# AFM tower on one core: the first tile's store, and the second tile's gathers, held until two steps have been multiplied

## The chip, the cores and the metric

The kernel runs on one core of one Trainium2 chip. The metric is the device time of one execution in microseconds (us); lower is better. The profile is of one execution of its own, so each reading of a trace is set against the time of that execution.

## What is computed

There are 1024 samples with 33 fields. Each field's id picks a row of 128 numbers from the field's own table. All 528 pairs of fields are multiplied elementwise, projected by a 128 x 128 matrix, put through a relu and reduced to one score a pair; a softmax over the pairs weighs the pair products, and a small MLP with three matrices follows. Cut to what matters:

```python
e = jnp.stack([tbl_0[ids[:, 0]], ..., tbl_32[ids[:, 32]]], axis=1)     # 1024 x 33 x 128, float32
row, col = np.triu_indices(33, k=1)
inner = e[:, row] * e[:, col]                                          # 1024 x 528 x 128
fm = relu(einsum('bpd,ad->bpa', inner, attn_W) + attn_b)
attn = softmax(einsum('ba,bpa->bp', gnn_feature, fm), axis=1)
pooled = einsum('bp,bpd->bd', attn, inner) * 100.0
h = concatenate([gnn_feature, pooled, gnn_feature], axis=1)
h = relu(h @ W_top1 + b_top1)
h = relu(h @ W_top2 + b_top2)
y = h @ W_top3
```

## The kernel before, in words

The 1024 samples are cut into eight tiles of 128 samples, and a tile into 32 steps of 4 samples: 256 steps in all. Steps are what the engines are busy with from about a twentieth of the time on.

**Rows of a tile.** GpSimd issues 33 indirect DMAs a tile (`gather(t)`, L280), one a field, each of which puts 128 rows of 512 bytes into `x_rows`. They are in five chunks c of 8, 8, 8, 8 and 1 fields, each with its own semaphore. Before a chunk of tile t > 0 is gathered, GpSimd waits until the tile before has been transposed out of that part of `x_rows` (`s_xt_done`) and until the rows of the tile before have been stored (`s_store`, 16 a store). SyncE stores all of `x_rows`, 2112 KB, to `x_dram` in device memory once all five chunks have landed (`store_rows(t)`, L230). TensorE turns a chunk over, field by field (`transpose_x(t, c)`, L620), ScalarE copies the result into `xt` (L347), and for the first two chunks copies it once more within `xt` (L337). There is one `x_rows`, and two halves of `xt`, used by turns.

**A step S.** VectorE writes 2112 columns of pair products (`product(S)`, L418). ScalarE rounds most of them to a short form (`round_inner`, L316), VectorE subtracts it to get the rest (`rest_of_inner`, L423). TensorE multiplies the 2112 columns in five chunks (`hidden(S)`), one or two of them in full precision (L580) and the others in three passes of parts (L587, L588, L589); steps 0 and 1 have four and three chunks in full precision. Each finished chunk adds 1 to `s_hidden`, so a step adds `CHUNKS`, which is 5. ScalarE applies the relu, two chunks at a time (L308). Every second step TensorE reduces two steps of `fm` to scores (L610, 32 matmuls). Products have four buffers: `product(S)` waits for `hidden(S - 4)`.

**Other work** of a tile is spread over the steps of the next by fixed lists: at steps 7, 10, 13 and 16 the weighted sums of the tile before (`fields`, L634, which read `x_fields`, loaded by SyncE from `x_dram`, and `attn_t`, spread by SyncE), at steps 18, 20, 22, 24 and 26 the transposes of the tile after (L620), at 19, 21 and 23 the MLP.

**The start.** Tile 0 has nothing before it: its five chunks are gathered, transposed and copied, and `product(0)` on VectorE waits for the last copy (`s_xt_out`). Then the steps begin.

**SyncE's queue**, in order: loads of ids, weights and biases; `store_rows(0)`; `store_rows(1)`; a wait for the first store and eight loads of `x_fields` (L219) for tile 0; then for each tile, as its attention gets ready, eight spreads of `attn_t` (L224), loads and spreads of the other two quarters, `store_rows(t + 2)`, and the loads for tile t + 1.

Of the kernel before, what the change touches and what calls it, by code (L numbers as in the profile page):

```python
# [12 lines left out]
def afm_tower(nc, gnn, ids, tables, w1, b1, w2, b2, w3, attn_w, attn_b, out):  # L13
# [12 lines left out]
    CHUNKS = 5  # L26
# [24 lines left out]
    FIELDS_AT = (7, 10, 13, 16)  # L51
    XT_AT = (18, 20, 22, 24, 26)
    MLP_AT = (19, 21, 23)
    MAX_AT, EXP_AT, INV_AT, SCALE_AT, TURN_AT = 1, 2, 2, 3, 4


# [8 lines left out]
    def jobs_of(S):  # L65
# [4 lines left out]
        if s in XT_AT and t + 1 < T:  # L70
            jobs.append(("x_t", t + 1, XT_AT.index(s)))
        if s in MLP_AT and t > 0:
            jobs.append(("mlp", t - 1, MLP_AT.index(s)))
        if S in LAST_FIELDS_AT:
# [12 lines left out]
    with ctx:  # L87
# [6 lines left out]
        def sem(name):  # L94
            return ctx.enter_context(nc.semaphore(name))
# [61 lines left out]
        s_hidden = sem("hidden_ready")  # L157
# [37 lines left out]
        def fields_in(c):  # L195
            return min(FU, F - FU * c)
# [16 lines left out]
        @block.sync  # L213
        def _(sp):
            def load_fields(t, c, dst, signal):
                for q in range(QS):
                    first = t * P + QS * FN * c + q
                    rows = x_dram[first:first + QS * (FN - 1) + 1:QS, 1:F, :]
                    sp.dma_start(dst[q * I:(q + 1) * I], rows.rearrange("n f d -> f n d")).then_inc(signal, 16)  # L219

            def spread_attn(c):
                for q in range(QS):
                    own = slice(q * I, (q + 1) * I)
                    sp.dma_start(attn_t[own, c % 2, q], attn_turned[own, c * FN:(c + 1) * FN, :])\  # L224
                        .then_inc(s_spread[c % 2], 16)

            def store_rows(t):
                for c in range(XJ):
                    sp.wait_ge(s_gather[c], 16 * fields_in(c) * (t + 1))
                sp.dma_start(x_dram[t * P:(t + 1) * P, :, :], x_rows[:]).then_inc(s_store, 16)  # L230

            sp.dma_start(ids_all[:], ids.rearrange("(t p) f -> p t f", p=P)).then_inc(s_ids, 16)
            sp.dma_start(attn_w_rows, attn_w).then_inc(s_small, 16)
            sp.dma_start(gnn_rows, gnn.rearrange("(t p) a -> p t a", p=P)).then_inc(s_small, 16)
            sp.dma_start(attn_b_sb[:], attn_b.rearrange("(a n) -> a n", n=1), allow_slow_non_contiguous=True).then_inc(s_small, 16)
            sp.dma_start(w1_sb[:], w1[0:2 * P, :].rearrange("(k p) n -> p k n", p=P)).then_inc(s_weights, 16)
            sp.dma_start(h1[:].rearrange("p m b -> p (m b)"), w1[2 * P:3 * P, :]).then_inc(s_weights, 16)
            sp.dma_start(w2_sb[:], w2.rearrange("(k p) n -> p k n", p=P)).then_inc(s_weights, 16)
            sp.dma_start(w3_sb[:], w3.rearrange("(k p) n -> p (k n)", p=P), allow_slow_non_contiguous=True).then_inc(s_weights, 16)
            sp.dma_start(b1_sb[:], b1.rearrange("(m p) -> p m", p=P), allow_slow_non_contiguous=True).then_inc(s_weights, 16)  # L240
            sp.dma_start(b2_sb[:], b2.rearrange("(m p) -> p m", p=P), allow_slow_non_contiguous=True).then_inc(s_weights, 16)
            store_rows(0)
            store_rows(1)
            sp.wait_ge(s_setup_t, 2)
            sp.wait_ge(s_store, 16)
            load_fields(0, 0, x_fields[:, 0], s_fields[0])
            load_fields(0, 1, x_fields[:, 1], s_fields[1])
            for t in range(T - 1):
                sp.wait_ge(s_inv, 3 * (t + 1))
                spread_attn(0)  # L250
                spread_attn(1)
                for c in (2, 3):
                    sp.wait_ge(s_fields_done, FJ * t + c - 1)
                    load_fields(t, c, x_fields[:, c % 2], s_fields[c % 2])
                    spread_attn(c)
                if t + 2 < T:
                    store_rows(t + 2)
                sp.wait_ge(s_store, 16 * (t + 2))
                for c in (0, 1):
                    sp.wait_ge(s_fields_done, FJ * t + c + 3)  # L260
                    load_fields(t + 1, c, x_fields[:, c], s_fields[c])
            sp.wait_ge(s_inv, 3 * T)
            spread_attn(0)
            spread_attn(1)
            sp.wait_ge(s_fields_done, FJ * (T - 1) + 1)
            load_fields(T - 1, 2, x_fields[:, 0], s_fields[0])
            spread_attn(2)
            sp.wait_ge(s_fields_done, FJ * (T - 1) + 2)
            load_fields(T - 1, 3, x_fields[:, 1], s_fields[1])
            sp.wait_ge(s_out, 16 * T)  # L270
# [135 lines left out]
        def _(dve):  # L406
# [123 lines left out]
            for S in range(ALL):  # L530
                t, s = divmod(S, STEPS)
                if S + 1 < ALL:
                    rest_of_inner(S + 1)
                weighs = [job for job in (jobs_of(S - 1) if S > 0 else []) if job[0] == "fields"]
                for _, of, c in weighs:
                    weigh(of, c)
                if part_at(S, TURN_AT) is not None:
                    turn_attn(part_at(S, TURN_AT))
                if S + 3 < ALL:
                    if (S + 3) % STEPS == 0:  # L540
                        dve.wait_ge(s_xt_out, XJ * (t + 2))
                        dve.wait_ge(s_repeat, K // FU * (t + 2))
                    product(S + 3)
                for _, of, c in weighs:
                    sum_weighted(of, c)
                if part_at(S, MAX_AT) is not None:
                    row_max(part_at(S, MAX_AT))
                if s == MAX_AT and t > 0:
                    gnn_block(t)
                if part_at(S, INV_AT) is not None:  # L550
                    invert_sum(part_at(S, INV_AT))
# [170 lines left out]
```

## Time and profile before

| | us |
|---|---|
| median of 3 runs | 1270.39 |
| lowest and highest | 1270.38, 1270.89 |
| the profiled execution | 1270.63 |
| its span, first to last instruction | 1268.2 |
| TensorE busy | 1201.0 (95%) |
| VectorE busy | 1147.9 (91%) |
| ScalarE busy | 1018.7 (80%) |
| GpSimd busy | 451.8 (36%) |

Times in the rows are microseconds from the span's start. A row of the order of time gives start, duration, engine, line, operation, output and inputs, shapes and a count (merged instructions); in brackets it gives how long the engine had been idle before, and what released it. SPq is SyncE issuing a DMA, PE is TensorE, PEld its weight loads, DVE VectorE, ACT ScalarE, POOL GpSimd. The ends of matmuls are modelled by the profiler, not observed. "remote" is the page's name for a releaser that it could match to no instruction.

### The profile page before, as it was taken

The numbers are of one execution on the slowest core, as the hardware profiler recorded it, in microseconds if no ns is written. First come the engines' busy times: TensorE is split into PE (matmuls) and PEld (weight loads), VectorE is DVE, ScalarE is ACT, GpSimd is POOL, SyncE is SP. The second block draws the span as 40 slices with busy tenths as digits, with TensorE's granted clock in tenths as the row PEclk, the third lists the DMA queues.
The fourth block names the chain that finished last, engine by engine and source line by source line (L and its number), as shares of the span: only waits on it lengthen the run. The fifth ranks groups of instructions, "written<-read, shape, count | busy, mean of one in ns | idle before, by whom it ended". The sixth has DMA issues, their size and how long they took to land.

```text
span 1268.2 us, 20736 instructions
## 1 busy us (share of the span) xinstructions
PE 1201.0 (95%) x8732; PEld 898.7 (71%) x8732; DVE 1147.9 (91%) x649; ACT 1018.7 (80%) x1039; POOL 451.8 (36%) x270
## 2 busy tenths in 40 slices
PE   1499999999999999999999999999999999999998
PEld 1267676777777777777777777677777777777766
DVE  2399899998999989999899989999799998999994
ACT  1288898778987889878897798978888788887883
POOL 6587684018800386005840088201880000000000
PEclk9999999999999999999999999999999999999999
DMA  4211410311103111131101311031110300011001
GB/s 108 97 34 50 105 32 26 102 45 30 34 13 125 31 32 28 30 106 37 32 20 47 106 27 32 20 111 39 30 34 21 117 18 1 1 29 39 17 9 38
DMA packets 54859, 58.83 MB, mean 46 GB/s; under 512 B 10728, under 2 KB 49136, under 8 KB 53744
## 3 DMA queue, kind: packets, MB, share of 16 engines
q1 hardware_dynamic: 46304, 40.20, 10.4%
q0 software_dynamic: 8448, 17.32, 5.2%
q8 instruction: 69, 1.13, 0.4%
q14 instruction: 22, 0.18, 0.0%
q10 hardware_dynamic: 16, 0.00, 0.0%
HBM read 36.12 MB, written 17.31 MB: 42 GB/s over the span
## 4 chain that ended last, share of the span: by engine, by line
PE 83%; ACT 8%; issue 4%; DVE 2%; POOL 2%; another core or an unknown queue 1%; DMA 1%; SPq 0%; ACTq 0%; DVEq 0%; POOLq 0%
PE scores L610 19%; PE ring L580 17%; PE ring L587 13%; PE ring L589 12%; PE ring L588 12%; PE ring L634 4%; ACT fm L308 3%; ACT inner_hi L316 3%; PE ring L620 2%; POOL x_rows L280 2%; PE ring L654 1%; DVE products L418 1%; ACT exp_pairs L323 1%; PE ring L648 1%
## 5 line engine op out<-in xcount | busy, mean ns | idle before, releaser
L308 ACT ACTIVATE fm<-ring,attn_b_sb 128x848 f32<-128x848 f32 (+1 forms) x640 | 597.2, 971 | 183.1 <-PE ring L580 174.3
L418 DVE TENSOR_TENSOR products<-xt 128x2112 f32<-128x2112 f32 x256 | 601.9, 2351 | 37.1 <-ACT xt L347 37.1
L280 POOL DMA_INDIRECT x_rows<-in_tbl,ids_all x264 | 451.1, 1709 | 498.2 <-PE ring L620 408.3
L423 DVE TENSOR_TENSOR low_parts<-products,inner_hi 128x1688 fp32r<-128x1688 f32 (+4 forms) x256 | 467.1, 1825 | 57.1 <-ACT inner_hi L316 56.0
L587 PE MATMUL ring<-inner_hi,attn_wt_lo 128*128 128x424 f32 (+1 forms) x971 | 433.1, 446 | 5.1 <-ACT fm L308 5.1
L316 ACT CAST inner_hi<-products 128x1688 fp32r<-128x1688 f32 (+4 forms) x256 | 392.3, 1532 | 5.2 <-DVE products L418 5.2
L589 PE MATMUL ring<-inner_hi,attn_wt_hi 128*128 128x424 f32 (+1 forms) x971 | 344.1, 354 | 0.0
L588 PE MATMUL ring<-low_parts,attn_wt_hi 128*128 128x424 f32 (+1 forms) x971 | 343.7, 354 | 0.0
L580 PE MATMUL ring<-products,attn_wt 128*128 128x424 f32 (+1 forms) x618 | 275.8, 542 | 10.0 <-issue 6.4
L610 PE MATMUL scores<-fm,gnn_blocks 128*32 128x264 f32 x4096 | 254.6, 389 | 6.5 <-ACT exp_pairs L323 6.4
L587 PEld LDWEIGHTS ring<-inner_hi,attn_wt_lo 128*128 128x128 f32 x971 | 182.6, 188 | 70.8 <-issue 37.6
L588 PEld LDWEIGHTS ring<-low_parts,attn_wt_hi 128*128 128x128 f32 x971 | 183.0, 188 | 43.5 <-issue 40.1
L610 PEld LDWEIGHTS scores<-fm,gnn_blocks 128*32 128x32 f32 x4096 | 120.0, 109 | 107.7 <-issue 13.8
L589 PEld LDWEIGHTS ring<-inner_hi,attn_wt_hi 128*128 128x128 f32 x971 | 182.4, 188 | 5.2
L580 PEld LDWEIGHTS ring<-products,attn_wt 128*128 128x128 f32 x618 | 104.6, 190 | 85.4 <-issue 78.2
L620 PE MATMUL ring<-ident,x_rows 128*128 128x128 f32 x264 | 39.2, 292 | 34.0 <-DMA x_rows<-in_tbl,ids_all 31.1
L634 PE MATMUL ring<-attn_t,x_fields 128*128 128x128 f32 x512 | 62.5, 275 | 2.0 <-ACT attn_t L401 1.4
L634 PEld LDWEIGHTS ring<-attn_t,x_fields 128*128 128x128 f32 x512 | 61.8, 191 | 3.2 <-issue 3.1
L347 ACT COPY xt<-ring 128x1024 f32<-128x1024 f32 (+1 forms) x40 | 38.5, 964 | 31.3 <-PE ring L620 15.7
L620 PEld LDWEIGHTS ring<-ident,x_rows 128*128 128x128 f32 x264 | 33.0, 151 | 39.4 <-DMA x_rows<-in_tbl,ids_all 25.7
L473 DVE TENSOR_TENSOR attn<-ring,xt 128x1024 f32<-128x1024 f32 x30 | 36.6, 1220 | 2.8 <-PE ring L634 2.8
L481 DVE TENSOR_REDUCE pooled<-attn 128x32 f32<-128x1024 f32 x30 | 36.5, 1216 | 0.1
(53 smaller groups left out, 203.9 us busy)
## 6 DMA issues: line engine op xcount, KB each, us to landing
x_dram<-x_rows SPq DMA_DIRECT2D x8, 2112.0 KB, 6.6
x_fields<-x_dram SPq DMA_DIRECT2D x128, 128.0 KB
x_rows<-in_tbl,ids_all POOLq DMA_INDIRECT x264
attn_t<-attn_turned SPq DMA_DIRECT2D x124, 32.0 KB, 1.9
w_sb<-in_W_top SPq DMA_DIRECT2D x2, 512.0 KB
x_fields<-in_r_gnn_feature SPq DMA_DIRECT2D x1, 512.0 KB
h<-in_W_top SPq DMA_DIRECT2D x1, 256.0 KB
ids_all<-in_ids SPq DMA_DIRECT2D x1, 132.0 KB, 2.7
```

Of the source, the lines that this page charges most:

```text
L280: nc.gpsimd.indirect_dma_start(out=x_rows[:, f, :], out_offset=None, in_=tables[f], in_offset=bass.IndirectOffsetOnAxis(ap=ids_all[:, t, f ...
L308: nc.scalar.activation(dst, slot(("hidden", pair, j))[:, :, 0:n], ACT.Relu, bias=attn_b_sb[:, 0:1]).then_inc(s_fm, 1)
L316: nc.scalar.copy(inner_hi[:, S % HI_BUFS, 0:COLS - at], plain[:, S % INNER_BUFS, at:]).then_inc(s_hi, 1)
L418: nc.vector.tensor_tensor(dst, a, b, ALU.mult).then_inc(s_inner, 1)
L423: nc.vector.tensor_tensor(inner[:, S % INNER_BUFS, at:end], plain[:, S % INNER_BUFS, at:end], inner_hi[:, S % HI_BUFS, 0:end - at].bitcast ...
L580: nc.tensor.matmul(dst, attn_wt[:], plain[:, S % INNER_BUFS, begin:end], start=True, stop=True)\
L587: nc.tensor.matmul(dst, attn_wt_lo[:], hi, start=True, stop=False)
L588: nc.tensor.matmul(dst, attn_wt_hi[:], lo, start=False, stop=False)
L589: nc.tensor.matmul(dst, attn_wt_hi[:], hi, start=False, stop=True).then_inc(s_hidden, 1)
L610: last = nc.tensor.matmul(scores[I * j:I * j + I, h, 0:HALF], block_of(s, j), fm[:, S % FM_BUFS, at:at + HALF], start=s == 0, stop=s == ST ...
L620: last = nc.tensor.transpose(to[:, n // 4, n % 4 * P:(n % 4 + 1) * P], x_rows[:, FU * c + n, :], ident[:])
L634: last = nc.tensor.matmul(bank[:, h, to:to + QS * I], x[:, n, :], own[:, :, n, :], start=True, stop=True)
```

## The change

One constant and one wait. SyncE, before it looks at the gathers of tile 0, waits until `s_hidden` has reached 10, that is, until all ten chunks of steps 0 and 1 have been multiplied. Everything behind that wait in SyncE's queue is behind it too: the first two stores and the loads of `x_fields` for tile 0. The gathers of tile 1 wait for the first store in GpSimd's queue and move with it. Nothing is added to any other engine, and no instruction is removed.

```diff
@@ -51,6 +51,7 @@
     FIELDS_AT = (7, 10, 13, 16)
     XT_AT = (18, 20, 22, 24, 26)
     MLP_AT = (19, 21, 23)
+    QUIET = 2
     MAX_AT, EXP_AT, INV_AT, SCALE_AT, TURN_AT = 1, 2, 2, 3, 4
 
 
@@ -239,6 +240,7 @@
             sp.dma_start(b2_sb[:], b2.rearrange("(m p) -> p m", p=P), allow_slow_non_contiguous=True).then_inc(s_weights, 16)
+            sp.wait_ge(s_hidden, CHUNKS * QUIET)
             store_rows(0)
             store_rows(1)
             sp.wait_ge(s_setup_t, 2)
```

## Rows read from the trace of the kernel before

**Rows 1.** The page's chain that ended last, and its tenths of busy time.

```profile
PE   1499999999999999999999999999999999999998
DVE  2399899998999989999899989999799998999994
...
PE 83%; ACT 8%; issue 4%; DVE 2%; POOL 2%; another core or an unknown queue 1%; DMA 1%; SPq 0%; ACTq 0%; DVEq 0%; POOLq 0%
```

**Rows 2.** The chain of waits in order of time, 39 to 76 us: start, us, what.

```profile
39.08 11.84 another core or an unknown queue
50.92 1.35 ACT xt L347 x2
52.29 4.63 DVE products L418 x2
...
60.64 2.28 DVE products L418
62.95 1.61 ACT inner_hi L316
64.56 0.87 ACT fm L308
67.46 1.92 PE scores L610 x32
...
75.61 1.92 PE scores L610 x32
```

**Rows 3.** TensorE in order of time: bursts of transposes, first steps.

```profile
15.86 1.94 PE L620 MATMUL ring<-ident,x_rows 128*128 128x128 f32 x8 [6.65 <-DMA x_rows<-in_tbl,ids_all]
26.07 1.97 PE L620 MATMUL ring<-ident,x_rows 128*128 128x128 f32 x8 [8.28 <-DMA x_rows<-in_tbl,ids_all]
35.99 1.97 PE L620 MATMUL ring<-ident,x_rows 128*128 128x128 f32 x8 [7.95 <-DMA x_rows<-in_tbl,ids_all]
46.19 2.18 PE L620 MATMUL ring<-ident,x_rows 128*128 128x128 f32 x9 [8.22 <-DMA x_rows<-in_tbl,ids_all]
...
54.75 5.12 PE L580 MATMUL ring<-products,attn_wt 128*128 128x424 f32 x8 [6.38 <-issue]
...
60.28 2.28 PE L580 MATMUL ring<-products,attn_wt 128*128 128x416 f32 x6
...
63.36 0.35 PE L589 MATMUL ring<-inner_hi,attn_wt_hi 128*128 128x424 f32 x1
...
65.47 0.46 PE L587 MATMUL ring<-inner_hi,attn_wt_lo 128*128 128x424 f32 x1 [0.34 <-ACT fm L308]
```

**Rows 4.** ScalarE in order of time: the copies into `xt`.

```profile
17.84 1.08 ACT L347 COPY xt<-ring 128x1024 f32<-128x1024 f32 x1 [3.80 <-issue]
...
28.08 1.08 ACT L347 COPY xt<-ring 128x1024 f32<-128x1024 f32 x1 [8.01 <-PE ring L620]
...
38.00 1.08 ACT L347 COPY xt<-ring 128x1024 f32<-128x1024 f32 x1 [7.68 <-PE ring L620]
50.91 1.35 ACT L347 COPY xt<-ring 128x1024 f32<-128x1024 f32 x2 [11.83 <-remote]
```

**Rows 5.** SyncE and GpSimd in order of time: stores, loads, first and last gathers of tiles 1, 2.

```profile
47.43 0.34 SPq L230 DMA_DIRECT2D x_dram<-x_rows  x1
...
54.63 3.11 POOL L280 DMA_INDIRECT x_rows<-in_tbl,ids_all  x1 [8.88 <-DMA x_dram<-x_rows]
58.04 2.46 POOL L280 DMA_INDIRECT x_rows<-in_tbl,ids_all  x1 [0.30 <-issue]
60.81 2.91 POOL L280 DMA_INDIRECT x_rows<-in_tbl,ids_all  x1 [0.30 <-issue]
...
71.80 1.52 POOL L280 DMA_INDIRECT x_rows<-in_tbl,ids_all  x1 [0.30 <-issue]
...
121.12 1.96 POOL L280 DMA_INDIRECT x_rows<-in_tbl,ids_all  x1 [0.30 <-issue]
...
124.70 0.33 SPq L230 DMA_DIRECT2D x_dram<-x_rows  x1
125.14 6.88 SPq L219 DMA_DIRECT2D x_fields<-x_dram  x8
...
134.50 0.94 POOL L280 DMA_INDIRECT x_rows<-in_tbl,ids_all  x1 [11.42 <-PE ring L620]
...
203.31 4.67 POOL L280 DMA_INDIRECT x_rows<-in_tbl,ids_all  x1 [0.30 <-issue]
...
281.54 2.37 POOL L280 DMA_INDIRECT x_rows<-in_tbl,ids_all  x1 [73.56 <-PE ring L620]
```

**Rows 6.** Stretches of the first store: engines, clock, DMA share, GB/s.

```profile
core 0: us, PE busy (x) PEld busy (x) DVE busy (x) ACT busy (x) POOL busy (x), PEclk, DMA share, GB/s
48.20:50.90 2.70, 0.17 (x1) 0.00 (x0) 0.00 (x0) 0.00 (x0) 0.00 (x0) 1.00 1.11 469
```

**Rows 7.** The same view for two later stores, in full stride.

```profile
248.50:255.10 6.60, 6.60 (x54) 4.62 (x53) 6.60 (x5) 5.33 (x7) 0.00 (x0) 1.00 0.80 333
398.60:405.20 6.60, 6.60 (x54) 4.62 (x53) 6.60 (x5) 5.33 (x7) 0.00 (x0) 1.00 0.81 333
```

**Rows 8.** VectorE in order of time: the same product of tiles 1, 2 and 7.

```profile
199.84 2.35 DVE L418 TENSOR_TENSOR products<-xt 128x2112 f32<-128x2112 f32 x1
...
349.81 2.35 DVE L418 TENSOR_TENSOR products<-xt 128x2112 f32<-128x2112 f32 x1
...
1099.82 2.35 DVE L418 TENSOR_TENSOR products<-xt 128x2112 f32<-128x2112 f32 x1
```

**Rows 9.** TensorE in order of time: transposes for tile 1.

```profile
133.20 1.03 PE L620 MATMUL ring<-ident,x_rows 128*128 128x128 f32 x8
...
143.67 1.06 PE L620 MATMUL ring<-ident,x_rows 128*128 128x128 f32 x8 [0.76 <-ACT fm L308]
```

**Rows 10.** `x_rows` and `x_dram`: transposes' range of starts, issue to landing up to 140 us.

```profile
L620 PE MATMUL ring<-ident,x_rows x66: 270/361/475, 15.9 to 172.2; 128*128 128x128 f32 x66
...
DMA to landing us min/median/max: 6.4/7.2/8.0
```

**Rows 11.** Weighted sums for tile 0: TensorE's matmuls and the spreads, range of starts.

```profile
L634 PE MATMUL ring<-attn_t,x_fields x48: 270/275/275, 228.5 to 258.8; 128*128 128x128 f32 x48
L224 SPq DMA_DIRECT2D attn_t<-attn_turned x16: 512/590/603, 216.0 to 247.7; - x16
```

## The prediction

> **What bounds the kernel now.** I read the page's chain that ended last first [rows 1]: 83% of it is TensorE, and the tenths show both TensorE and VectorE at 9 in nearly every slice after the second. A change to one store and to gathers can only matter if it moves the moment at which this dense part begins, or disturbs it. So I went on to the chain in order of time [rows 2]. Up to 39 us it is gathers and the transposes behind them; then come 11.84 us put down to "another core or an unknown queue", then ScalarE's last two copies into `xt`, then VectorE's first products. The reader is to see the odd entry: there is no other core, and the copies should be waiting for the transposes.
>
> TensorE and ScalarE in order of time show what is hidden in it. In the first three bursts of eight transposes ScalarE starts 0.04 us after the modelled end: 15.86 + 1.94 = 17.80 and 17.84, 26.07 + 1.97 = 28.04 and 28.08, 35.99 + 1.97 = 37.96 and 38.00 [rows 3, 4]. The fourth burst has nine, the eighth of which should end at 46.19 + 1.97 = 48.16, so the copy is due at 48.20. It starts at 50.91, released by "remote" [rows 4]. **2.71 us are lost** there, and only there. In those 2.7 us every engine is idle but the DMA engines, which run at 469 GB/s: this is the first store, issued at 47.43 [rows 5, 6]. 47.43 is the only store that meets the end of a burst of transposes.
>
> From `product(0)` at 52.29 VectorE does not wait again in the opening, and through product 3, the rounding and a relu it leads to TensorE's restart at 65.47, after which TensorE is dense: reductions at 67.46 and 75.61 [rows 2, 3]. So a shift of 52.29 is a shift of everything.
>
> **Does such a shift survive to the end?** The same product of tiles 1, 2 and 7 starts at 199.84, 349.81 and 1099.82 [rows 8]: 149.97 us for one tile and 750.01 / 5 = 150.00 for each of the next five, although tiles 1 to 6 have gathers in them and the last one has no more to fetch. No step in the dense part waits for a fixed moment; what is won at 52.29 is won at the end. By the same rows gathers and stores in full stride cost nothing measurable.
>
> **The change, part by part.**
>
> The added wait itself: one instruction on SyncE, which has been waiting anyway; nothing runs on it but issues. Zero, hidden behind the loads of the start, and the issue of a store is no busy time of another engine.
>
> The store of tile 0 leaves 47.43. If it is what held the transposes' result back, the copy starts at 48.20, `product(0)` at 52.29 - 2.71 = 49.58, TensorE at 54.75 - 2.71 = 52.04. The gain is 2.71 us. Below, it is bounded by nothing (0, the stall is not the store's); above, by what an earlier start of TensorE could bring besides. TensorE's first eight full-precision matmuls take 5.12 us, 0.64 each, and the next six 2.28 us, 0.38 each [rows 3]: it is at 1.2 GHz first and at 2.4 GHz from about 59 us on. Shifted by 2.71 us it may rise sooner or later against the work. That moves TensorE by about 1 us either way (three or four matmuls at 0.64 in place of 0.38), but what it restarts on at 65.47 is ScalarE's relu, fed by VectorE [rows 2, 3], with 0.34 us to spare. So I allow 0.7 us of further gain and 0.7 us of loss, and take 0 as the likeliest.
>
> The store now starts when step 1 is multiplied. The last matmul of step 1 ends at 63.36 + 0.35 = 63.71 now [rows 3], at 61.0 after the shift. It lands 6.4 to 8.0 us later [rows 10], under steps 2 and 3. What does it cost there? Two later stores in full stride have TensorE and VectorE busy 6.60 of 6.60 us [rows 7]: zero. I take this, the nearest row, with one doubt, priced below.
>
> The gathers of tile 1 begin 54.63 - 47.43 = 7.20 us after the store's issue now [rows 5], so at 68.2, up to 69.8 for a slow landing: 14 to 15 us later. Eight of them end at 71.80 + 1.52 = 73.3 now, 88 at the latest; the first transposes of tile 1 want them at 133.20 - 2.7 = 130.5 [rows 5, 9]. All 33 end at 121.12 + 1.96 = 123.1 now, at 134 to 138 then (the first three take 3.11, 2.46 and 2.91 beside 1.5 to 2 of the later ones, so some of the delay is made good); the fifth chunk is wanted at 172.2 - 2.7 = 169.5 [rows 5, 10]. Spare time over 30 us: zero.
>
> Behind it in SyncE's queue: `store_rows(1)` goes from 124.70 to about 136 to 140, and the eight loads of `x_fields` with it, from 125.14 [rows 5]. They are wanted at 228.5 [rows 11]. Zero. The spreads that are queued behind start at 216.0 [rows 11], far later. In GpSimd's queue the gathers of tile 2 now wait for `store_rows(1)` to land, at 143 to 148 instead of 134.50; their last, 203.31, goes to 212 to 220 [rows 5], and they are wanted by transposes that end at 281.5 [rows 5]. Zero. `store_rows(2)` is held by SyncE's own order, and its window at 248.5 is far behind the gathers. From tile 2 on the schedule is the old one, 2.71 us earlier.
>
> **The sum**, against the profiled execution: 1270.63 - 2.71 = 1267.92. That execution is 0.24 above the median of the runs shown, so in medians 1270.39 - 2.71 = 1267.7. A measurement of this kernel can tell about 0.2% from no change, 2.54 us; the forecast gain is just above that.
>
> The Trainium skill speaks against the cause that I assume: its page "SBUF — State Buffer", in "SBUF: two separate sides", says that engine ports and DMA ports are disjoint, so that a DMA can't be slowed by a compute operation nor the other way round, and that TensorE and ScalarE never wait on anyone. Rows 7 agree with it, rows 6 look as if they did not. By that rule the sum would be 1270.4, no change. Its page "Perfetto Trace Analysis", in "Tensor Engine Instruction (MATMUL, LD_WEIGHTS)", adds that a matmul's end is estimated and that the semaphore goes out only when the write has been acknowledged; so the 48.16 above is a model, and 50.91 the first real sign of the end.
>
> **The rivals.**
>
> *The stall is not the store's and stays.* For it: two stores in full stride disturb nothing [rows 7], and the onset is one coincidence. Against it: three bursts without a store have 0.04 us, the one with a store 2.75 [rows 3, 4]. Time 1270.4 (1269.9 to 1270.9).
>
> *The stall moves with the store.* What is hit may be a burst of transposes of `x_rows` while `x_rows` is being stored, which happens nowhere else now. After the change it happens again: the store of tile 1, issued at 136 to 140 and moving data for some five us, lies across the second burst of tile 1, 143.67 - 2.7 = 141.0 [rows 5, 9], or the first store hits TensorE in steps 2 and 3. Then 2.71 us are won and up to 2.71 lost again: 1269.5 to 1270.4, take 1270.2.
>
> *Slower: only the new collision costs.* The first stall has another cause and stays, and the store of tile 1 holds the second burst by 2.71 us, with ScalarE's copy and the ring buffers behind it: 1270.39 + 2.71 = 1273.1. It decides this way if that store's data are still moving at the end of the burst, near 142, and if TensorE has no slack there; it had 0.76 us of idle before that burst [rows 9], so 1.9 to 2.7 us: 1272.3 to 1273.1.
>
> **How the numbers follow.** Forecast, stall gone: 0.50. Stall stays: 0.30, since the nearest rows in full stride clear the store. Moved: 0.11. Slower: 0.09. In the forecast's own range of 1267.0 to 1268.4 about three quarters lie beyond 2.54 us, so faster by over 0.2% gets 0.38, and the rest of it, 0.12, joins stays and moved: 0.53. The range that leaves out the slower case and the outer edges of the others is 1267.0 to 1270.9.
>
> **What would show it right or wrong.** In the changed kernel's trace: the entry for an unknown queue in the chain shrinks from 11.84 to about 9.1 us; the fourth `xt` copy starts near 48.2 and `product(0)` near 49.6; the first store is issued near 61, first gather of tile 1 near 68, second store at 136 to 140; the same product of tile 1 at about 197.1 in place of 199.84. If the copy still starts near 50.9, the stall was not the store's. If `product(0)` is early but the product of tile 1 is not, the loss came back: look then at TensorE's idle time at 61 to 68 and at the burst at 141. If TensorE is later than VectorE's products allow at 52 to 66, the clock's rise was mis-sized.

## The result: 17 us slower, and the profile after

| | before | after |
|---|---|---|
| median of 5 runs | 1270.39 | 1287.73 |
| lowest and highest | 1270.35, 1271.75 | 1283.56, 1288.44 |
| the profiled execution | 1270.63 | 1283.56 |
| its span | 1268.2 | 1281.1 |
| TensorE busy | 1201.0 (95%) | 1205.7 (94%) |
| VectorE busy | 1147.9 (91%) | 1147.9 (90%) |
| GpSimd busy | 451.8 (36%) | 482.1 (38%) |

The change makes the kernel 17.3 us slower in medians, a ratio of 1.0137. The recorded comparison of the runs, which doesn't go by the medians, has 1.0124, with an interval of 1.0112 to 1.0135. Slower it is by either. The executions of the changed kernel lie at 1283.6 to 1283.9 (two) and at 1287.7 to 1288.4 (three). The profiled one is of the first kind, so its trace shows 12.9 us of span, and the further 4 us of the others stay unexplained. Line numbers after are one or two higher than before.

The page, its tenths and its chain, where [rows 1] stand for before:

```profile
PE   1499799999999999999999999999999999999998
...
DVE  2399689998999989999899989999899998999994
...
PEclk9999899999999999999999999999999999999999
...
PE 78%; issue 8%; ACT 8%; POOL 5%; DMA 1%; DVE 1%; ACTq 0%; POOLq 0%; DVEq 0%
```

One slice, the fifth (128 to 160 us), has lost work on both engines and has a lower granted clock. "Issue" has grown from 4% to 8% and GpSimd from 2% to 5% of the chain, while the entry for an unknown queue has gone: the end now hangs on GpSimd for a while. What follows is in order of time, in the form of [rows 4], [rows 5] and [rows 9] (start, duration, engine, line, operation, what it works on, idle time before it and who ended that). ScalarE, the third and fourth copies:

```profile
41.36 1.08 ACT L349 COPY xt<-ring 128x1024 f32<-128x1024 f32 x1 [11.03 <-remote]
51.19 1.35 ACT L349 COPY xt<-ring 128x1024 f32<-128x1024 f32 x2 [8.75 <-remote]
```

SyncE, both stores (merged into one row; the second is issued at 177.81) and the loads behind them:

```profile
64.21 113.93 SPq L231 DMA_DIRECT2D x_dram<-x_rows  x2
...
178.24 6.85 SPq L220 DMA_DIRECT2D x_fields<-x_dram  x8
```

GpSimd, the first three gathers of tile 1 and the last:

```profile
72.05 43.05 POOL L282 DMA_INDIRECT x_rows<-in_tbl,ids_all  x1 [26.33 <-DMA x_dram<-x_rows]
115.40 1.59 POOL L282 DMA_INDIRECT x_rows<-in_tbl,ids_all  x1 [0.31 <-issue]
117.30 1.96 POOL L282 DMA_INDIRECT x_rows<-in_tbl,ids_all  x1 [0.30 <-issue]
...
174.62 1.53 POOL L282 DMA_INDIRECT x_rows<-in_tbl,ids_all  x1 [0.30 <-issue]
```

TensorE, bursts of transposes for tile 1:

```profile
133.47 1.03 PE L622 MATMUL ring<-ident,x_rows 128*128 128x128 f32 x8
...
149.50 1.97 PE L622 MATMUL ring<-ident,x_rows 128*128 128x128 f32 x8 [6.68 <-DMA x_rows<-in_tbl,ids_all]
...
165.44 1.94 PE L622 MATMUL ring<-ident,x_rows 128*128 128x128 f32 x8 [1.16 <-ACT fm L310]
```

Three things are to be seen.

First, with no store in flight the fourth copy into `xt` still starts at 51.19, released by "remote", and now the third one is late as well (41.36 against 38.00 before). So a stall of that size needs no store.

Second, the store is issued at 64.21, the first gather of tile 1 starts at 72.05, and **that one gather lasts 43.05 us** where it took 3.11. It ends at 115.10. From there the gathers go at the old pace, and the last of tile 1 ends at 174.62 + 1.53 = 176.15, where it was 121.12 + 1.96 = 123.08 [rows 5]: 53.1 us late, 14 of which I had allowed.

Third, the second burst of transposes for tile 1 starts at 149.50 in place of 143.67 [rows 9], after 6.68 us of idle time that a gather ended.

The loss lies in one place. VectorE's products of steps 0 to 20 start 0.27 to 0.30 us later than before, that of step 24 is 0.07 us earlier, that of step 28 is 13.20 us later, and that of step 228 is 13.65 later. Stretches of the time in which the gather hangs, and of the loss behind it (columns: stretch, length, busy time of each engine with its number of instructions, granted clock, share of the DMA engines, GB/s), before:

```profile
72.00:114.00 42.00, 42.00 (x303) 30.69 (x302) 42.00 (x23) 36.38 (x37) 35.60 (x22) 1.00 0.13 35
...
146.00:162.00 16.00, 15.24 (x103) 11.34 (x96) 13.40 (x7) 14.55 (x15) 14.17 (x7) 1.00 0.09 26
```

and after:

```profile
72.00:114.00 42.00, 42.00 (x303) 30.86 (x302) 42.00 (x22) 36.41 (x36) 41.95 (x1) 1.00 0.00 1
...
130.00:146.00 16.00, 12.82 (x86) 9.82 (x84) 13.96 (x8) 15.04 (x15) 13.87 (x8) 0.96 0.11 30
146.00:162.00 16.00, 11.32 (x65) 7.48 (x65) 5.08 (x3) 4.40 (x4) 12.95 (x11) 0.72 0.15 41
162.00:182.00 20.00, 17.64 (x126) 12.48 (x125) 14.84 (x7) 16.48 (x16) 12.02 (x8) 0.91 0.29 106
```

From 72 to 114 us GpSimd is inside one instruction (x1 where there were 22) and nothing moves (1 GB/s where it was 35), while TensorE, VectorE and ScalarE are as busy as before to within a tenth of a microsecond. The bill comes at 130 to 182 us. TensorE waits for the late rows from 142.82 to 149.50, and its granted clock falls to 0.50, the lower of its two levels (1.2 GHz), inside that wait: it is 0.50 in every stretch of 2 us from 145 to 155, then 1.00 again (0.98 in the first such stretch), and 0.58 and 0.57 in the two from 165 to 169, after 6 us in which TensorE was busy for 4.1. In the table above that is 0.04, 0.28 and 0.09 of 16, 16 and 20 us, doubled: about 14 us at half speed. The same bursts show it: eight transposes in 1.97 us at 149.50, 1.06 us in [rows 9].

### The profile page after: what moved, and what is told of

It is laid out like the page before. It is cut to its first block, busy times and chain, and to the rows that moved or that the text cites. A ratio compares the mean times of both kernels' runs of the same rounds, so it can differ in the third digit from the quotient of the medians.

```text
span 1281.1 us, 20737 instructions
## 1 busy us (share of the span) xinstructions
PE 1205.7 (94%) x8732; PEld 900.8 (70%) x8732; DVE 1147.9 (90%) x649; ACT 1019.5 (80%) x1039; POOL 482.1 (38%) x270
## 4 chain that ended last, share of the span: by engine, by line
PE 78%; issue 8%; ACT 8%; POOL 5%; DMA 1%; DVE 1%; ACTq 0%; POOLq 0%; DVEq 0%
PE scores L612 18%; PE ring L582 16%; PE ring L589 12%; PE ring L591 11%; PE ring L590 11%; POOL x_rows L282 5%; PE ring L636 4%; ACT fm L310 3%; ACT inner_hi L318 3%; PE ring L622 2%; PE ring L656 1%; ACT exp_pairs L325 1%; PE ring L650 1%; DMA x_dram<-x_rows 1%; DMA x_rows<-in_tbl,ids_all 1%
## 5 line engine op out<-in xcount | busy, mean ns | idle before, releaser
L282 POOL DMA_INDIRECT x_rows<-in_tbl,ids_all x264 | 481.4, 1823 | 481.5 <-PE ring L622 363.5
```

The costliest lines, as they stand in the source:

```text
L282: nc.gpsimd.indirect_dma_start(out=x_rows[:, f, :], out_offset=None, in_=tables[f], in_offset=bass.IndirectOffsetOnAxis(ap=ids_all[:, t, f ...
```

## The experiments

**What a gather waits for.** The trace of before holds a pattern that the prediction passed over. VectorE in order of time, before:

```profile
66.48 1.92 DVE L423 TENSOR_TENSOR low_parts<-products,inner_hi 128x1696 fp32r<-128x1696 f32 x1
68.32 2.35 DVE L418 TENSOR_TENSOR products<-xt 128x2112 f32<-128x2112 f32 x1
70.59 1.91 DVE L423 TENSOR_TENSOR low_parts<-products,inner_hi 128x1688 fp32r<-128x1688 f32 x1
72.41 2.35 DVE L418 TENSOR_TENSOR products<-xt 128x2112 f32<-128x2112 f32 x1
```

and GpSimd beside it, before:

```profile
65.42 1.96 POOL L280 DMA_INDIRECT x_rows<-in_tbl,ids_all  x1 [0.30 <-issue]
67.68 1.53 POOL L280 DMA_INDIRECT x_rows<-in_tbl,ids_all  x1 [0.30 <-issue]
69.52 1.97 POOL L280 DMA_INDIRECT x_rows<-in_tbl,ids_all  x1 [0.31 <-issue]
71.80 1.52 POOL L280 DMA_INDIRECT x_rows<-in_tbl,ids_all  x1 [0.30 <-issue]
```

The gathers end at 67.38, 69.21, 71.49 and 73.32: each 0.89 to 0.91 us after a start on VectorE. With VectorE idle one takes 0.94 us in all; GpSimd, a gather of tile 0, before:

```profile
44.80 0.94 POOL L280 DMA_INDIRECT x_rows<-in_tbl,ids_all  x1 [0.30 <-issue]
```

The gather at 134.50 in [rows 5] takes 0.94 us too, and there VectorE starts an instruction in the same moment (134.51). So a gather issued beside VectorE's steps seems to get its turn where one VectorE instruction gives way to the next. All of those instructions read two operands from SBUF, and a gather reads its row numbers from `ids_all` in SBUF. The Trainium skill's page "SBUF — State Buffer", in "Who interferes with whom", names just this pair: a VectorE instruction with two inputs in SBUF contends with a GpSimd instruction that reads SBUF. By its section "SBUF: two separate sides", whoever starts first has the shared ports for the whole instruction. The rows agree, within a turn of 1.5 to 2 us. The 43.05 us, across more than 20 VectorE instructions, are not in that rule. What decides whether the gather gets a turn?

The times of before differ by the chip that a kernel ran on, so each run is set against before on its own chip.

**Where the store is put, and whether the store is needed at all.** Three runs (before: 1267.21). `quiet1` holds the store for one step, `quiet4` for four; `gathers_alone` leaves the store at its old place and holds only the gathers:

```diff
-    QUIET = 2
+    QUIET = 1
```


> The changed kernel with the hold cut to one step instead of two (5 chunks). Break theory: the first gather of tile 1 gets through only when VectorE makes its first break, which both traces have near 114 us; it starts near 68 us, takes some 46 us, ends near 115 as in the changed kernel, and the time is the same 1283 to 1288 us. Delay theory (the loss grows with the length of the hold): the gather ends some 4 us sooner, 1279 to 1284 us.

```diff
-    QUIET = 2
+    QUIET = 4
```


> The changed kernel with the hold doubled to four steps (20 chunks). Break theory: the gather starts near 80 us, takes only some 35 us, and ends near 115 again: 1283 to 1288 us, no more than with two steps. Delay theory: everything 8 us later than with two steps, 1291 to 1296 us.

```diff
                 for c in range(XJ):
+                    if t == 1 and c == 0:
+                        pool.wait_ge(s_hidden, 2 * CHUNKS)
```


> The kernel before with its store at the old place near 47.4 us; only GpSimd waits for two steps (10 chunks) before the first gather of tile 1. Break theory: the gather starts near 64 us and hangs to 115 us: 1283 to 1288 us. Store theory (the late store under steps 2 and 3 is what holds GpSimd): the gather takes 2 to 3 us as before, 1270 to 1271 us.

Measured: 1285.93 (ratio 1.0149, 1.0132 to 1.0166), 1285.49 (1.0146, 1.0129 to 1.0163) and 1285.23 (1.0143, 1.0126 to 1.0159). GpSimd in order of time, the first gather of tile 1, in `quiet1`:

```profile
65.05 46.72 POOL L282 DMA_INDIRECT x_rows<-in_tbl,ids_all  x1 [19.52 <-DMA x_dram<-x_rows]
```

in `quiet4`:

```profile
76.85 34.99 POOL L282 DMA_INDIRECT x_rows<-in_tbl,ids_all  x1 [31.32 <-DMA x_dram<-x_rows]
```

and in `gathers_alone`:

```profile
62.13 50.18 POOL L282 DMA_INDIRECT x_rows<-in_tbl,ids_all  x1 [16.09 <-PE ring L591]
```

Holding the gathers alone costs what the change costs. The gathers are the cause, and the store's place is not. And whenever it is asked for, the first gather ends at the same moment: 111.77, 111.84 and 112.31, which is 62.5 us behind VectorE's first product in each (49.25, 49.32, 49.79); in the changed kernel 115.10 - 52.57 = 62.5 too. So something in VectorE's sequence opens the door there, and waiting longer for the store even shortens the gather.

**A store in the middle of the steps.** `second_store`: before, and at 61.60 us another store of the same size, out of `xt`, so that the gathers are not touched (here and below, allocations of buffers and semaphores are left out of the diffs):

```diff
             store_rows(0)
+            sp.wait_ge(s_hidden, 2 * CHUNKS)
+            sp.dma_start(spare[:, :], xt[:, 0].rearrange("p b f -> p (b f)")[:, 0:F * D]).then_inc(s_spare, 16)
             store_rows(1)
...
+                if t == 2 and c == 0:
+                    act.wait_ge(s_spare, 16)
```


> The kernel before with store and gathers at their old places, and one more store of the same size, out of the first half of xt into a spare tensor, once two steps are multiplied (near 64 us). Break theory: a store there costs nothing, 1270 to 1271 us. Store theory: the gathers that are under way hang or TensorE stalls, 1275 us or more.

Measured 1267.36 (1.0001, 0.9991 to 1.0011). A store under steps 2 and 3 costs nothing, as the prediction had it from [rows 7].

**Letting the gather in.** Three ways, on one chip (before: 1270.49), each in the changed kernel. `pause`: VectorE waits in step 4 until the first gather is through. `short_op`: VectorE gets a memset of one column there and no wait; it reads nothing from SBUF. `awake`: while it would be still, GpSimd issues 11 extra gathers into a spare tile, so that it is in turn without a break.

```diff
+                        if t == 1 and f == 0:
+                            nc.gpsimd.memset(mark[:], 0.0).then_inc(s_in, 1)
...
+                if S == 4:
+                    dve.wait_ge(s_in, 1)
```


> The changed kernel, and VectorE stops once, in step 4 (near 74 us), until GpSimd has issued the first gather of tile 1. Break theory: the stop is a break by itself; the gather ends within 2 us of it instead of near 115, VectorE loses under 3 us where it has reserve, the last gather of tile 1 lands near 140, and the time is that of the kernel before within 1 us. If something else holds the gather (its ring, its code, a transfer), VectorE waits for it to the end: some 40 us longer than before.

```diff
+                if S == 4:
+                    nc.vector.memset(mark[:], 0.0)
```


> The changed kernel, and one VectorE memset of one column is put into step 4 (near 74 us), with no wait: VectorE stays without a break but one operation reads no operand from SBUF. If it is reading two operands without end that shuts GpSimd out, the gather ends here, near 75 to 77 us, and the time is that of the kernel before. If only real idle time of VectorE lets it in, nothing changes: end near 112 to 115 us, 18 us above before.

```diff
-            for t in range(T):
+            gather(0)
+            pool.wait_ge(s_xt_done, XJ)
+            for n in range(11):
+                nc.gpsimd.indirect_dma_start(
+                    out=dump[:, n, :], out_offset=None, in_=tables[0],
+                    in_offset=bass.IndirectOffsetOnAxis(ap=ids_all[:, 0, 0:1], axis=0),
+                ).then_inc(s_dump, 16)
+            for t in range(1, T):
                 gather(t)
```


> The changed kernel, and GpSimd issues 11 extra gathers into a spare tile between the end of tile 0 and the first gather of tile 1 (from about 48 to 70 us), so it is in turn with VectorE all the time. If a GpSimd that is in turn keeps getting its turn, the first gather of tile 1 takes 1.5 to 3 us, the last ends near 140 us and the time is that of the kernel before. If each batch of gathers anew needs a break, it hangs to 112 us: 18 us above before.

Measured: 1269.97 (0.9996, 0.9986 to 1.0005), 1270.05 (0.9997, 0.9988 to 1.0007) and 1269.96 (0.9996, 0.9986 to 1.0005). **Each of the three takes back the whole loss.** VectorE in order of time, `short_op`:

```profile
74.78 1.48 DVE L426 TENSOR_TENSOR low_parts<-products,inner_hi 128x1272 fp32r<-128x1272 f32 x1
74.81 0.06 DVE L536 MEMSET mark<- 128x1 f32 x1
76.18 2.36 DVE L421 TENSOR_TENSOR products<-xt 128x2112 f32<-128x2112 f32 x1
```

and GpSimd, its first two gathers of tile 1:

```profile
71.50 4.18 POOL L283 DMA_INDIRECT x_rows<-in_tbl,ids_all  x1 [25.90 <-DMA x_dram<-x_rows]
75.99 1.10 POOL L283 DMA_INDIRECT x_rows<-in_tbl,ids_all  x1 [0.31 <-issue]
```

The memset stands ahead of the low part in VectorE's program, though its row begins 0.03 us behind it. 0.06 us of work on VectorE at 74.81, and the gather is through at 71.50 + 4.18 = 75.68, 0.87 us later. The next one needs no help: once in turn, GpSimd gets nearly every boundary (before has 22 gathers beside 23 VectorE instructions in 72 to 114 us). In `awake` the first gather of tile 1, at 75.92, takes 1.09 us in the same place. The gathers of these kernels still end late (at 140.1 in `pause`, 139.6 in `short_op` and 142.4 in `awake`, where the prediction had 134 to 138), and their time is that of before: lateness of that size is free.

**How late may the request come?** `gathers_one_step`: before, and GpSimd waits until step 0 is multiplied:

```diff
                 for c in range(XJ):
+                    if t == 1 and c == 0:
+                        pool.wait_ge(s_hidden, CHUNKS)
```


> The kernel before with only GpSimd held, for one step (5 chunks) in place of two: the first gather of tile 1 would start some 8 us after VectorE's first product instead of 5 (gets in) or 12 (hangs). If the door shuts when VectorE stops waiting for others at its start, this finds on which side 8 us lies: either 3 us for the first gather and the time of before, or an end near 112 us and 18 us above before; nothing in between.

Measured 1270.35 (0.9999, 0.9990 to 1.0009). The gather is asked for at 60.32, 7.9 us after VectorE's first product, and takes 1.25 us. In `gathers_alone` it is asked for 12.3 us after it, and takes 50.18. A door closes in between.

**The empty operation or the wait?** The memset could have opened the door because it reads nothing, or because it drained something at an instruction boundary that any further instruction would drain. Two runs (before: 1266.84): `short_op_wait` gives the memset a wait that has long been met; `split_product` cuts step 8's product into two halves, two operands each, the second without a wait.

```diff
+                if S == 4:
+                    dve.wait_ge(s_hidden, 2 * CHUNKS)
+                    nc.vector.memset(mark[:], 0.0)
```


> The changed kernel with the same memset in step 4 as in the run that cured it, but now it waits for a semaphore that was met long before (10 chunks). Two theories of what let GpSimd in there. Operand theory: a VectorE operation that doesn't read two operands from SBUF lets it in; it still does: first gather ends near 75 to 77 us, time of before within 1 us. Wait theory: what shuts GpSimd out is an unbroken row of VectorE instructions that each carry a wait already met, and the first one without a wait lets it in; this one carries a wait, so the gather hangs to 112 to 115 us: 13 to 18 us above before.

```diff
+                if S == 8:
+                    half = GROUPS // 2
+                    x0, x1 = x[:, 0:half, :], x[:, half:GROUPS, :]
+                    for n, xh in enumerate((x0, x1)):
...
+                        last = nc.vector.tensor_tensor(dst[:, half * n:half * (n + 1)], a, b, ALU.mult)
+                    last.then_inc(s_inner, 1)
+                    return
```


> The changed kernel with the product of step 8 (near 80 us) cut into two multiplications of half the columns, the second of which waits for nothing; both read two operands from SBUF. Operand theory: nothing changes, the first gather hangs to 112 to 115 us: 13 to 18 us above before. Wait theory: it gets in at the second half and ends near 81 to 84 us, the last gather of tile 1 lands near 147, and the time is that of before within 1 us.

Measured: 1267.24 (1.0001, 0.9991 to 1.0010) and 1285.47 (1.0145, 1.0128 to 1.0162). The first gather of tile 1 on GpSimd, `short_op_wait`:

```profile
68.41 4.40 POOL L283 DMA_INDIRECT x_rows<-in_tbl,ids_all  x1 [22.64 <-DMA x_dram<-x_rows]
```

and `split_product`:

```profile
69.03 43.26 POOL L282 DMA_INDIRECT x_rows<-in_tbl,ids_all  x1 [23.07 <-DMA x_dram<-x_rows]
```

A memset opens with or without a wait. One more boundary, between two operations that both read two operands, does not open. So what matters is what kind of operation it is. Both memsets are also far shorter than either half of the product, and none of these runs has a tiny operation with two operands from SBUF, so that the missing operands are what opens is the likeliest reading and not shown by itself.

**Is the unbroken row the condition, or GpSimd's own stillness?** Three runs (before: 1267.25). `short_op_before` is the changed kernel with the memset in step 2, where it runs at 63.68, **before** the gather is asked for. `awake_short` is `awake` with 6 extra gathers in place of 11. `late_start` is before, with three reductions of one operand (19.87 us) on VectorE ahead of the first product, and the gathers held until the first product is done: GpSimd is still for 26 us, but VectorE's unbroken row of two-operand instructions is young.

```diff
+                if S == 2:
+                    nc.vector.memset(mark[:], 0.0)
```


> The changed kernel with the one-column memset two steps sooner, in step 2, near 66 us (63 on a chip without the late copies), 4 to 5 us before the first gather of tile 1 asks at 71.5 (68.4). Continuity theory (the door closes only when VectorE has gone some 8 to 12 us with nothing but operations of two operands, and stays shut until one that isn't, or until one that comes late): the memset starts the count anew, the gather gets in at once, 1 to 3 us, and the time is that of before. Opening-while-waiting theory (GpSimd gets in only through an opening that comes after it has asked): it hangs for 42 us, 13 to 18 us above before.

```diff
+            for n in range(6):
```


> The changed kernel with 6 extra gathers in place of 11: GpSimd then stands still from about 64 to 71 us, 7 to 8 us, while VectorE goes on with two-operand operations. Continuity theory: what counts is VectorE's row since GpSimd's last turn or the last other operation, 7 us, so the gather still gets in at once: time of before. If any pause of GpSimd in the dense stretch shuts it out, it hangs to 112 or 115 us: 13 to 18 us above before. GpSimd's pause as such being what counts (over 15 us shuts it out) also gives the time of before here.

```diff
+                    if t == 1 and c == 0:
+                        pool.wait_ge(s_inner, 1)
...
+            for n in range(3):
+                nc.vector.tensor_reduce(mark[:, n:n + 1], xt[:, 0], AX.XY, ALU.max)
             product(0)
```


> The kernel before with three reductions of xt on VectorE ahead of the first product, some 20 us, and GpSimd held until the first product is done. GpSimd then stands still for some 27 us, but asks 2.3 us after VectorE's row begins. Continuity theory: the gather gets in at once, 1 to 3 us, and the time is before plus the 20 us of the reductions, 1287 to 1292. Pause theory (a GpSimd that stood still for over 15 us is shut out): it hangs for some 60 us, to 62.5 us after the first product, and the time is 13 to 18 us more, 1301 to 1308.

`short_op_before`: 1267.37 (1.0001, 0.9991 to 1.0011). `late_start`: 1286.45 (1.0151), 19.2 us longer, which is no more than the 19.87 us put in front. The first gather of tile 1 on GpSimd, `short_op_before`:

```profile
68.35 2.15 POOL L283 DMA_INDIRECT x_rows<-in_tbl,ids_all  x1 [22.70 <-DMA x_dram<-x_rows]
```

and `late_start`:

```profile
71.77 2.82 POOL L283 DMA_INDIRECT x_rows<-in_tbl,ids_all  x1 [26.13 <-DVE products L421]
```

Both in at once, after 22.70 and 26.13 us of idleness on GpSimd, about that of the changed kernel (26.33). GpSimd's stillness is not the condition. The trace of before says the same: in [rows 5] the first gather of tile 2 is asked for at 281.54, after 73.56 us of stillness, and takes 2.37 us. VectorE had broken its row just before, with an operation of one operand (VectorE, before):

```profile
278.76 0.23 DVE L484 TENSOR_SCALAR pooled<-pooled 128x128 f32<-128x128 f32 x1
```

A memset 4.67 us ahead of the request is enough: what counts is how long VectorE has been issuing two-operand instructions without a break when the request comes. Whether that is a time or a number of instructions, these runs can't tell apart.

`awake_short` hit the edge. Its ten executions fall in two groups: 1284.83, 1284.77, 1285.27 and 1285.42, and six from 1266.65 to 1267.22 (ratio 1.0045, 1.0000 to 1.0090). The profiled one is of the longer group; GpSimd in order of time, its last extra gather and the first of tile 1:

```profile
61.18 1.08 POOL L298 DMA_INDIRECT dump<-in_tbl,ids_all  x1 [0.30 <-issue]
70.00 41.96 POOL L284 DMA_INDIRECT x_rows<-in_tbl,ids_all  x1 [7.75 <-DMA x_dram<-x_rows]
```

The last turn of GpSimd was at the boundary 0.9 us before 62.26, at 61.36; the request comes 8.6 us behind it, and is shut out four times in ten. The runs together, by the time from the start of VectorE's row (its first product, a memset, or GpSimd's last turn) to the request:

| run | us since the row began | first gather, us | it ends, us behind the first product |
|---|---|---|---|
| before | 2.3 | 3.11 | |
| `late_start` | 2.6 | 2.82 | |
| `short_op_before` | 4.7 | 2.15 | |
| `second_store` | 5.2 | 3.06 | |
| `gathers_one_step` | 7.9 | 1.25 | |
| `awake_short` | 8.6 | let in 6 times of 10, 41.96 in the profile | 62.5 |
| `gathers_alone` | 12.3 | 50.18 | 62.5 |
| `quiet1` | 15.8 | 46.72 | 62.5 |
| `xt_later` (below) | 18.9 | 43.64 | 62.5 |
| `split_product` | 19.3 | 43.26 | 62.6 |
| after | 19.5 | 43.05 | 62.5 |
| `quiet4` | 27.5 | 34.99 | 62.5 |

What opens the door at 62.5 us, where there is no memset, is not shown. The last boundary before it is the low part at 114.25 in the changed kernel, and it is the first whose rounded input came only just ahead of it: ScalarE ended that rounding at 112.62 + 1.60 = 114.22. In all seven kernels with a shut-out gather this lead is 0.03 or 0.04 us, and for every earlier low part it is 0.45 us or more. That would be a break in the row too short for a record of idle time; no run moved it.

**Is it the lateness that costs?** `xt_later`: the changed kernel, with the transposes for tile 1 at steps 20 to 28 in place of 18 to 26 (before: 1266.84).

```diff
+    def xt_at(t):
+        return tuple(s + 2 for s in XT_AT) if t == 0 else XT_AT
...
-        if s in XT_AT and t + 1 < T:
-            jobs.append(("x_t", t + 1, XT_AT.index(s)))
+        if s in xt_at(t) and t + 1 < T:
+            jobs.append(("x_t", t + 1, xt_at(t).index(s)))
```


> The changed kernel with the five chunks of transposes for tile 1 two steps later each (steps 20 to 28 in place of 18 to 26), 8 to 10 us. If the loss is the lateness of the gathers as these transposes see it, it shrinks by those 8 to 10 us, to 4 to 10 us above before. If it has another place (the clock, GpSimd's later batches, the loads of x_fields), it stays at 13 to 18 us.

Measured 1275.51 (1.0071, 1.0054 to 1.0088). The gather is shut out as in the changed kernel (43.64 us from 68.34), and the loss is 8.7 us in place of 18.0 to 18.7 in `quiet1`, `quiet4`, `gathers_alone` and `split_product`, on chips with the same time of before. TensorE in order of time, two of the bursts of this kernel:

```profile
164.68 1.97 PE L625 MATMUL ring<-ident,x_rows 128*128 128x128 f32 x8 [6.58 <-DMA x_rows<-in_tbl,ids_all]
...
176.83 1.09 PE L625 MATMUL ring<-ident,x_rows 128*128 128x128 f32 x8 [1.44 <-DMA x_rows<-in_tbl,ids_all]
```

Moving the consumer by two steps (9.4 us of the 150.0 a tile takes [rows 8], 150.0 / 32 x 2) moved the long wait for the gathers from the second burst (149.50) to the third and halved the loss. The shut-out itself cost nothing while it lasted (72 to 114 us above); it costs where its lateness runs past the transposes.

**And the late copies into `xt`?** Over all runs there are two kinds of chips. On one, before takes 1270.1 to 1270.5, and the fourth copy starts near 50.9, released by "remote"; on the other it takes 1266.8 to 1267.3, and the copy starts where the modelled end of the transposes has it, with the store at its old place. ScalarE in order of time, `second_store`:

```profile
47.87 1.35 ACT L354 COPY xt<-ring 128x1024 f32<-128x1024 f32 x2 [8.86 <-PE ring L627]
```

`fill_pe` asked whether TensorE's falling idle behind the last burst delays the sign of its end: before, with eight matmuls on the identity behind the transposes. `fill_pe`, `fill_pe2` and `fill_pe3` are the same kernel; the first two fell on chips without late copies: 1267.34 against 1266.84 and 1266.66 against 1267.25, which tell only that the eight matmuls cost nothing.

```diff
                 transpose_x(0, c)
+            for _ in range(8):
+                nc.tensor.matmul(scores[:, 0, 0:P], ident[:], ident[:], start=True, stop=True)
```


> The kernel before (no hold) with 8 matmuls of the identity behind the last transposes of tile 0, some 1.7 us of TensorE. On a chip that has the late fourth copy into xt (50.9 in place of 48.2 us): if the result of a burst is held back while TensorE stands still behind it, the copy starts near 48.3 and the time falls by 2.5 us; if not, it stays at 50.9 and the time is that of before. On a chip that doesn't have it, 0 to 0.5 us either way and nothing is told apart.

> Once more the kernel before with 8 matmuls of the identity behind the last transposes of tile 0, in case this chip has the late copies into xt (a time of before near 1270.4 and not 1267.2). If the result of a burst is held back while TensorE stands still behind it, the fourth copy starts near 48.3 us and the time falls by 2.5 us against before; if not, the copy stays near 51 and the time is that of before. On a chip without late copies it is the time of before and tells nothing.

`fill_pe3` came on the right kind (before: 1270.08): 1269.94 (0.9998, 0.9988 to 1.0007). Its transposes are followed by other work on TensorE, and the copy is as late as ever (ScalarE in order of time):

```profile
50.84 1.35 ACT L347 COPY xt<-ring 128x1024 f32<-128x1024 f32 x2 [11.53 <-remote]
```

> The kernel before, unchanged, for a trace on the same chip as the run with the 8 matmuls. The first gather of tile 1 asks 2 to 5 us after VectorE's first product and takes 2 to 4 us. The fourth copy into xt starts near 48.2 or near 51 us, with the time 1267.2 or 1270.4 to match; the store is at 47.4 us in either case, so a copy at 48.2 would show again that the store doesn't hold it.

`before_again`, the old kernel once more on that chip, has it at 50.88 and takes 1270.62. Neither the store nor TensorE's idling is the cause. What is, stays open. It goes with the 3.2 us between the two kinds of chips: VectorE's first product starts at 52.2 to 52.6 on the one and at 49.3 to 49.8 on the other.

## Why the prediction was wrong

**Where the stall at 48 us comes from** ("The store … is what held the transposes' result back", taken as the likeliest). Wrong. It rested on one coincidence, the only store that meets the end of a burst. The copy is late without a store (51.19 after) and on time with one (`second_store`, 47.87). The stall neither went nor moved with the store: `product(0)` is at 52.57 in place of the 49.6 forecast. The rule that I set against the cause, that transfers and engines don't meet at SBUF (the Trainium skill's page "SBUF — State Buffer", "SBUF: two separate sides"), was the better guide, and my 0.50 against 0.30 was the wrong way round.

**The store under steps 2 and 3**: zero, right. `second_store` measured it by itself.

**The gathers of tile 1** ("All 33 end at 121.12 + 1.96 = 123.1 now, at 134 to 138 then … Spare time over 30 us: zero"). This is the step that failed at the price of 17 us. The sum was nearly sound for what it assumed: the kernels in which the door is held open end their gathers at 139.6 to 142.4 and lose nothing. But it carried over a duration, 1.5 to 3 us a gather, from a trace in which GpSimd had asked 2.3 us after VectorE's first product, to a place 19.5 us after it. The gather then took 43.05 us, used up the 30 us of spare time, and the clock fell in TensorE's wait for it. I had looked at what the wait holds up, and not at what the moved instructions would meet in their new place. [Rows 5] had the hint: the first three take 3.11, 2.46 and 2.91 us beside 1.08 to 1.97 of the others of tile 1, and I wrote that down as time that may be made good instead of asking what a gather waits for.

**The rivals.** "Stays" had the stall right and the sum wrong. "Slower" had the sign, by a collision of the second store with a burst of transposes that doesn't occur, and was some 15 us too small. The true mechanism was on no list. The chances had a slip besides: the forecast's range of 1267.0 to 1268.4 has 0.85 of its 1.4 us beyond 2.54 us of gain, which is 61% if it is spread evenly and not three quarters.

**The shift that survives** [rows 8]: right, and it made the loss easy to place. The shift is 13.20 us at step 28 and 13.65 at step 228.

**TensorE's clock in the opening.** The two levels before and after 59 us were read from durations, 0.64 and 0.38 us a matmul [rows 3]. The granted clock of the trace reads 1.00 throughout 50 to 68 us, so it does not bear that out; nothing in the result hangs on it.

**The issue times**: store near 61, measured 64.21, as 61.0 assumed the 2.71 us gained; without them 63.7. First gather 72.05 against 68.2 to 69.8, again with the same 2.7 us in it; it came 7.84 us behind the store's issue, where I had 7.20. The second store was forecast at 136 to 140 and came at 177.81.

## What to carry to other kernels

Before GpSimd's instructions are moved, look at what VectorE runs at their new place. Here an indirect DMA on GpSimd, which reads its row numbers from SBUF, had to find its turn between VectorE instructions with two SBUF operands, and a duration taken from one place doesn't hold in another. If such a stretch is long and unbroken, let GpSimd ask early in it, or put one tiny operation without SBUF inputs on VectorE: here a memset of 0.06 us undid a loss of 17. A slack of 30 us is a statement about the durations that it was computed with, so ask what would make one of them ten times longer before it is booked as zero; and a stall that coincides once with a transfer has not been explained by it.

## What the runs showed of the hardware

A gather by indirect DMA on GpSimd took 0.94 us with VectorE idle and 1.08 to 3.11 us beside the two-operand instructions of up to 2.35 us before 125 us (trace of before). First asked for 12.3 to 27.5 us into an unbroken row of them, it took 35 to 50 us; at 7.9 us it was let in, and at 8.6 us in six of ten executions. The Trainium skill's page "SBUF — State Buffer", in "SBUF: two separate sides", has the lock last for one instruction; here GpSimd stayed shut out over 18 to 25 of them. Its section "Who interferes with whom" holds, marked as inferred, that an elementwise operation on two tensors leaves the making of descriptors alone; in seven kernels here a row of such operations held up an indirect DMA for 35 to 50 us.

VectorE lost nothing while it shut GpSimd out: 22 instructions in 42.00 us busy in the stretch above, and 23 before.

TensorE's granted clock fell to 0.50 inside a wait of 6.68 us and stayed there until about 155 us, and was low again for part of 165 to 169 us: eight transposes took 1.97 us at 149.50 and 1.03 at 133.47.

The same kernel took 1266.8 to 1267.3 us on some chips and 1270.1 to 1270.5 on others, and the difference lay in the opening: on the slower ones ScalarE starts 2.7 to 4.7 us behind the modelled end of a burst of transposes, in one or two of the first four bursts.
